# Adding the bias b1 with bfloat16 ones and three bfloat16 parts instead of two fp32r parts

## What is computed

```python
h = jnp.einsum('td,edf->etf', xt, W1) + b1[:, None, :]      # E = 8 experts, D = 128, F = 512
h = _layernorm(jax.nn.relu(h), g1, be1)
y = jnp.einsum('etf,efd->etd', h, W2) + b2[:, None, :]
y = _layernorm(jax.nn.relu(y), g2, be2)
gate = (jax.nn.one_hot(idx, E, dtype=x.dtype) * probs[..., None]).sum(axis=1)   # the two best experts
out = jnp.einsum('te,etd->td', gate, y)
```

## Time and profile before

| | |
|---|---|
| median of three runs | 625.96 us |
| lowest, highest | 620.47, 628.31 us |
| span of the profiled execution | 528.5 us |
| TensorE busy | 492.8 us (93%), mean granted clock 0.965 |
| VectorE busy | 451.7 us (85%) |
| ScalarE busy | 408.1 us (77%) |
| GpSimd busy | 379.2 us (72%) |

### The profile page before, as it was taken

One profiled execution on the slowest core, in us unless ns is written; L12 is line 12 of the kernel. 1 busy time (PEld: TensorE's weight loads), 2 busy tenths in 40 slices (PEclk: granted clock), 3 DMA queues, 4 the chain that ended last, 5 costly groups with the idle time before them and its releaser, 6 DMA issues. The chain is left out here.

```text
span 528.5 us, 15192 instructions
## 1 busy us (share of the span) xinstructions
PE 492.8 (93%) x3105; PEld 392.4 (74%) x3105; DVE 451.7 (85%) x2209; ACT 408.1 (77%) x1115; POOL 379.2 (72%) x523
## 2 busy tenths in 40 slices
PE   7899999999976989999999999989999999999953
PEld 6355666555545879999989889879888888989821
DVE  6778788799995668888999799989999889999887
ACT  7587787868754668888888788888888888888753
POOL 1637777777777776688856578786887777878781
PEclk9999999999985889999999999999999999999986
DMA  6970111155513365555555565665665666665765
GB/s 173 308 215 21 58 52 56 53 134 107 98 56 130 100 150 149 143 153 156 154 146 136 155 175 151 178 190 157 170 196 155 185 190 158 181 193 160 213 174 159
DMA packets 79358, 77.81 MB, mean 147 GB/s; under 512 B 11102, under 2 KB 72697, under 8 KB 79142
## 3 DMA queue, kind: packets, MB, share of 16 engines
q1 hardware_dynamic: 70854, 59.92, 44.5%
q0 software_dynamic: 8416, 16.93, 9.0%
HBM read 54.65 MB, written 22.59 MB: 146 GB/s over the span
## 5 line engine op out<-in xcount | busy, mean ns | idle before, releaser
L602 POOL DMA_INDIRECT expert_rows<-rows_ring,slot x128 | 123.6, 965 | 39.3 <-issue 37.5
L626 POOL DMA_INDIRECT expert_results<-y,target x119 | 118.7, 997 | 36.3 <-issue 35.2
L1530 PE MATMUL bank<-W,h2T 128*128 x1080 | 143.4, 276 | 1.2 <-ACT h2T L792 1.2
L1530 PEld LDWEIGHTS bank<-W,h2T 128*128 128x128 f32 x1080 | 131.9, 193 | 1.6 <-issue 1.6
L784 ACT ACTIVATE h1T<-bank 128x512 f32<-128x512 f32 x135 | 80.7, 598 | 44.7 <-PE bank L1512 42.9
L1287 DVE BATCH_NORM_STATS2 stf<-h1T 128x6 f32<-128x512 f32 x135 | 91.0, 674 | 0.1
L1518 PEld LDWEIGHTS bank<-ident,h1T 128*128 128x128 f32 x540 | 67.7, 141 | 18.7 <-issue 0.4
L1518 PE MATMUL bank<-ident,h1T 128*128 128x128 f32 x540 | 81.3, 273 | 0.0
L792 ACT ACTIVATE h2T<-bank 128x512 f32<-128x512 f32 x135 | 79.5, 589 | 0.1
L1509 PE MATMUL bank<-b_parts,onesr 128*128 x135 | 65.4, 484 | 2.6 <-DVE h3lo L1279 2.4
L701 ACT ACTIVATE n<-X,nm,rs 128x128 f32<-128x128 f32 x128 | 54.0, 483 | 9.0 <-DVE nm L1205 6.9
(11 more groups left out here) (237 smaller groups left out, 1062.2 us busy)
## 6 DMA issues: line engine op xcount, KB each, us to landing
shifts<-expert_shifts SPq DMA_DIRECT2D x119, 192.0 KB
hrow<-expert_rows SPq DMA_DIRECT2D x135, 65.0 KB, 3.0
xi<-expert_results SPq DMA_DIRECT2D x12, 512.0 KB, 5.2
out_x<-X SPq DMA_DIRECT2D x15, 256.0 KB
X<-in_L_attn_x SPq DMA_DIRECT2D x7, 512.0 KB, 7.3
shifts<-in_L_ffn_W SPq DMA_DIRECT2D x4, 512.0 KB, 7.0
expert_rows<-rows_ring,slot POOLq DMA_INDIRECT x128, 2.3
expert_results<-y,target POOLq DMA_INDIRECT x119
```

The lines of the kernel that those rows point to most:

```text
L602: nc.gpsimd.indirect_dma_start(out=rows_d, out_offset=bass.IndirectOffsetOnAxis(ap=slot[q][:, n // TOPK, n % TOPK:n % TOPK + 1], axis=0), ...
L626: nc.gpsimd.indirect_dma_start(out=results_d, out_offset=bass.IndirectOffsetOnAxis(ap=target[i % TARGETS][:], axis=0), in_=y[k], in_offset ...
L1530: ins = mm(acc, rT[q][:, ch * P:(ch + 1) * P], W2[:, bass.ds(e2 * CF + ch, 1), :], start=(ch == 0), stop=(ch == CF - 1))
```

## The change

The ones become the bfloat16 matrix `ones` that other products already use. The table `b1_parts` becomes bfloat16, and three of its rows are filled instead of two: b1 rounded to bfloat16, the rest rounded, and the rest of that, which together are b1 exactly. GpSimd clears the table in one instruction and makes the three parts in four, between its clearing of `b2_rows` and its wait for W1. ScalarE's ten instructions and VectorE's subtraction go. SyncE copies three rows of half the bytes instead of two.

```diff
-        b1hi = sb("b1hi", [E, F], F32R)
-        b1_parts = sb("b1_parts", [P, E, F], F32R)
-        onesr = sb("onesr", [P, P], F32R)
+        PARTS = 3
+        b1_part = [sb(f"b1_part_{n}", [E, F], BF16) for n in range(PARTS)]
+        b1_parts = sb("b1_parts", [P, E, F], BF16)
@@ sync
-            sp.wait_ge(dve_setup, SETUP_END)
-            sp.wait_ge(act_setup, 2)
             sp.wait_ge(b1_zeroed, 1)
-            sp.dma_start(b1_parts[0:1, :, :].bitcast(F32), b1hi[:].bitcast(F32)).then_inc(b1_stored, 16)
-            sp.dma_start(b1_parts[1:2, :, :].bitcast(F32), b1lo[:].bitcast(F32)).then_inc(b1_stored, 16)
+            sp.wait_ge(b1_step, 4)
+            for n in range(PARTS):
+                sp.dma_start(b1_parts[n:n + 1, :, :], b1_part[n][:]).then_inc(b1_stored, 16)
@@ gpsimd
             nc.gpsimd.memset(b2_rows, 0.0).then_inc(b2_zeroed, 1)
+            nc.gpsimd.memset(b1_parts[:].rearrange("p e f -> p (e f)"), 0.0).then_inc(b1_zeroed, 1)
+            pool.wait_ge(gains_loaded, 48)
+            nc.gpsimd.tensor_copy(b1_part[0][:], b1f[:]).then_inc(b1_step, 1)
+            pool.wait_ge(b1_step, 1)
+            nc.gpsimd.tensor_tensor(b1_rest[:], b1f[:], b1_part[0][:], ALU.subtract).then_inc(b1_step, 1)
+            pool.wait_ge(b1_step, 2)
+            nc.gpsimd.tensor_copy(b1_part[1][:], b1_rest[:]).then_inc(b1_step, 1)
+            pool.wait_ge(b1_step, 3)
+            nc.gpsimd.tensor_tensor(b1_part[2][:], b1_rest[:], b1_part[1][:], ALU.subtract).then_inc(b1_step, 1)
@@ scalar
-            act.wait_ge(dve_setup, SETUP_PADDING)
-            for e in range(E):
-                ins = nc.scalar.activation(b1_parts[:, e, :], padding[:, 0:1].broadcast_to([P, F]), ACT.Copy)
-            ins.then_inc(b1_zeroed, 1)
-            def split_b1():
-                act.wait_ge(gains_loaded, 48)
-                act.wait_ge(dve_setup, SETUP_PADDING)
-                nc.scalar.activation(b1hi[:], b1f[:], ACT.Copy).then_inc(act_setup, 1)
-                nc.scalar.activation(onesr[:], onesf[:], ACT.Copy).then_inc(act_setup, 1)
@@ vector, at the end of gains_setup
-                dve.wait_ge(act_setup, 2)
-                mark(vec.tensor_tensor(b1lo[:], b1f[:], b1hi[:], ALU.subtract))
-                assert done[0] == SETUP_END
@@ tensor
-                    mm(h, onesr[:], b1_parts[:, bass.ds(e, 1), :], start=True, stop=False)
+                    mm(h, ones[:], b1_parts[:, bass.ds(e, 1), :], start=True, stop=False)
```

More of the change, by code:

```diff
@@ L140, in adaln_ssm_moe_kernel @@
         scan = [sb(f"scan_{q}", [P, L]) for q in range(2)]
-        spare_gb = [sb("spare_gb_0", [P, L]), sb("spare_gb_1", [P, L], F32R)]
+        spare_gb = [sb(f"spare_gb_{q}", [P, L]) for q in range(2)]
         b1f = spare_gb[0][0:E, :]
-        b1lo = spare_gb[1][0:E, :]
+        b1_rest = spare_gb[1][0:E, :]
         assert L == F
@@ L247, in adaln_ssm_moe_kernel @@
         shift_rows += [of[:, n * 3 * D:(n + 1) * 3 * D] for of in (xi_flat[1], mix_flat) for n in range(2)]
-        shift_rows += [scan[0][:, 0:3 * D], scan[1][:, 0:3 * D], spare_gb[0][:, 0:3 * D], spare_gb[1][:, 0:3 * D].bitcast(F32)]
+        shift_rows += [scan[0][:, 0:3 * D], scan[1][:, 0:3 * D], spare_gb[0][:, 0:3 * D], spare_gb[1][:, 0:3 * D]]
         def ring(i):
@@ L276, in adaln_ssm_moe_kernel @@
         early_gb = [t[:, :].rearrange("p (j d) -> p j d", j=J) for t in scan]
-        second_gb = [t[:, :].bitcast(F32).rearrange("p (j d) -> p j d", j=J) for t in spare_gb]
+        second_gb = [t[:, :].rearrange("p (j d) -> p j d", j=J) for t in spare_gb]
         idle_rows = rows_ring[:].rearrange("p k j r -> p (k j r)")
@@ L303, in adaln_ssm_moe_kernel @@
         gb_stored, gb_loaded, b1_stored = sem("gb_stored"), sem("gb_loaded"), sem("b1_stored")
+        b1_step = sem("b1_step")
         (n1_ready, t1_done, h1T_ready, xi0_done, xi1_done, xi0_ready, xi1_ready, z_done,
@@ L478, in load_shifts @@
                 if i == SLOTS:
-                    sp.wait_ge(b1_stored, 32)
+                    sp.wait_ge(b1_stored, 16 * PARTS)
                 if last_user(i) is not None:
@@ L743, in mixer_step @@
                     normalise(s - 1, n2[1 - q], 0, rs[q], nm[q], range(J // 2, J)).then_inc(n2_ready, 1)
-                if isinstance(s, int) and s == -1:
-                    split_b1()
             run(mixer_step, FIRST1)
@@ L1484, in _ @@
             pe.wait_ge(w1lo_ready, E // W1E)
-            pe.wait_ge(b1_stored, 32)
+            pe.wait_ge(b1_stored, 16 * PARTS)
             pe.wait_ge(table_ready, 1)
@@ L1544, in _ @@
                 mm(late_total[b], ident[:], late_gb[b], start=False, stop=True).then_inc(late_total_done, 1)
-SETUP_PADDING, SETUP_CT, SETUP_MOD, SETUP_GB, SETUP_MIX, SETUP_SUMS, SETUP_END = 2, 3, 4, 8, 12, 13, 14
+SETUP_PADDING, SETUP_CT, SETUP_MOD, SETUP_GB, SETUP_MIX, SETUP_SUMS = 2, 3, 4, 8, 12, 13
 _INS = ['L0_attn_x', 'L0_attn_Win', 'L0_attn_bin_', 'L0_attn_Bp', 'L0_attn_Cp', 'L0_attn_Dp', 'L0_attn_Wout',
```

## The result

The changed kernel takes 630.88 us (median of 10 runs, 626.32 to 637.67), the kernel before 623.69 us (10 runs, 616.60 to 628.31), each run on the same chip. The ratio is 1.0122, 95% interval [1.0087, 1.0157]: some 7.6 us slower, where 1.9 us less were forecast. It is too little for the 2% bound, but it has a sign, and the sign is the other one. Medians here are over all runs of a kernel, ratios and their intervals over its fast runs alone, so that the two need not divide out.

What follows compares the result with a forecast made beforehand. TensorE's products were taken to set the 2.37 us tile period. Product -2.6, waits for rows +0.4 and setup overlap +0.3 sum to -1.9 us against 625.96: 624.1 us (chance 0.73), range 619.5 to 628.1.

Steps and rivals of the forecast that it cites:

- the 2% bound: Whole kernel's time: the change this measurement can tell from none, about 2%, 12.5 us.
- so the work is hidden with 1.3 us to spare: Setup: GpSimd's b1 work ends by 15.4 us, before W1's first cast at 16.71, so it costs nothing there.
- GpSimd's subtractions run beside VectorE's small serial chain: Setup: overlap with VectorE's chain from about 14.67 to 15.4 us costs 0.3 us, bounds 0 to 0.8.
- the setup slips by more than I allow: Setup: what follows if GpSimd's small instructions take twice their price; no size given.
- The product: Expert loop: bfloat16 b1 product saves 16 ns, its weights 3 ns, on each of 135 tiles, 2.6 us.
- the extrapolation from 8 and 32 columns: Expert loop: 0.42 ns a column carried on to 512 columns gives 377 ns for bfloat16 against 393 for fp32r.
- Rival (a): Expert loop: bfloat16 streams no faster in a group with fp32r products; nothing saved, setup costs 0.3, 626.3 us; chance 0.18.
- (b): Expert loop: the b1 product gets much shorter, 13.8 us go, time 612.9 us, just over 2% faster; chance 0.04.
- (c): Expert loop: changing type exposes the next weight load, 0.19 us 135 times, 25.7 us slower, 651 us; chance 0.05.
- What arrives of it: Expert loop: of the product's 2.6 us saving, growing waits for DMA rows take back 0.4 us, TensorE's address instruction zero.
- Waits for rows that grow: Expert loop: some five DMA waits each grow by up to 0.15 us, 0 to 0.8 us, taken as 0.4.

Runs made afterwards that it cites:

- GpSimd's part alone: Kernel before with its fp32r product and two parts, but GpSimd clears the table and does four instructions on b1: 536.25 us, ratio 1.0128.
- its third trace: Trace of the kernel before, run unchanged once more as a sample of TensorE's start: 622.34 us, ratio 1.0074 against itself.
- four products: Product of ones and b1 issued four times a tile, two pairs: fp32r 1.1308 and 1.1188, bfloat16 1.1211 and 1.1080 against the kernel before.
- the product alone: Kernel before with the three-part bfloat16 product, ScalarE clearing and rounding, VectorE subtracting, nothing added to GpSimd: 531.59 us, 1.0038; on another chip 624.63 us, 1.0104.
- the fp32r kernel with four products: Kernel before with its fp32r product of ones and b1 issued four times a tile; second taking 698.56 us, ratio 1.1188.
- the kernel before taken again: Kernel before, unchanged, against itself: 530.78 us, ratio 1.0005.
- the changed kernel with the wait: Changed kernel in which GpSimd's first split of W1 also waits for VectorE's norms of batches 1 and 2: first 629.03 us, 0.9956; again 533.18 us, 1.0042.
- The product alone with the wait: Bfloat16 product with nothing of b1 on GpSimd, and W1's first split also waiting for VectorE's norms, against the kernel before: ratio 0.9984.

## Why the prediction was wrong

**The step that failed** is "so the work is hidden with 1.3 us to spare", on GpSimd's five instructions. It asked when GpSimd's own queue is next needed, and by that it was right (b1 done at 14.36, the cast at 17.14). It did not ask who else is held while GpSimd works. The one place where it did, "GpSimd's subtractions run beside VectorE's small serial chain", took the chain at its old time and 0.3 us for the overlap. The clearing held one VectorE instruction by 2.3 us, b1's subtractions held others, the chain began 3.1 us late, and once late it lay under W1's split, 1.43 + 2.76 us a pair. The price was 6.8 us (4.6 to 8.9), as GpSimd's part alone shows, not 0.3, bounds 0 to 0.8. The last sentence ("the setup slips by more than I allow") came nearest, but for another reason: GpSimd's instructions on b1 took 0.60 and 1.15 us, less than the 0.7 and 1.6 forecast and not twice as much, and the setup slipped all the same.

The prediction had the row for it: VectorE's 0.57 at 24.92, more than three times the 0.17, under this subtraction in the trace of before:

```profile
22.67 2.78 POOL L592 TENSOR_TENSOR W1lo<-shifts,W1hi 128x256 fp32r<-128x256 f32 x4
```

It asked this only of b1's instructions, and not whether the chain stays clear of W1's split. That was the narrow place: the chain ended at 16.5, 0.2 us ahead of a cast at 16.71. The kernel before itself is caught there in its third trace, with the late start: the chain runs from 15.16 to 18.41 us, the cast starts at 16.20, and the steps behind it take 0.31 us. A chain that clears such a neighbour by 0.2 us turns a small delay into a large one.

Under a GpSimd clearing, which reads nothing, VectorE's one-input `TENSOR_SCALAR` was held to its end, while a `BATCH_NORM_AGGREGATE` under it took its 0.38 us. The Trainium skill has this in SBUF — State Buffer, section "Who interferes with whom": the two engines share a pair of ports, `tensor_scalar` may take it whole, and whoever comes second is blocked, not slowed. The trace agrees (2.50 us under the one clearing, 3.53 under a second). The prediction did not weigh this rule, and it speaks against this change.

**The product.** 16 ns from the type and 3 from the weights were forecast; the runs show 18 and some 2, and 20 to 22 ns off the period by the two ways of reading it, 2.7 to 3.0 us in all. That step held, and so did the extrapolation from 8 and 32 columns. Rival (a), no faster in the group, is refuted by the period; (b) and (c) too. (With (c)'s 25.7 us the time would be 651.7, not 651.) The product's row became shorter by far more (0.38 against 0.48), as its wait had moved to the next row.

**What arrives of it** was taken at 2.2 of 2.6 us, and stays open. With four products all of the gain shows in the loop. With one, GpSimd's part with and without the new product gave the same ratio (1.0128 and 1.0127, each known to 0.004, which leaves their difference open by 3 us to either side), and the product alone was 0.4% slower. In the traces of the first kind of chip the loop takes 327.8, 328.2 and 324.9 us with the fp32r product, and 325.2, 324.7, 326.1, 325.7, 327.3 and 326.5 us with the other: 1.1 us less on average, not 2.7 to 3.0. Waits for rows that grow would do this, and the forecast had 0.4 us for them. But the spread within one kind is as large as the difference, the last four of the six come from a chip without a trace of the other product, and no run that loads rows differently was made.

**Open.** The product alone should then be even or 1 to 2 us faster, and its first comparison says 0.1 to 0.7% slower. Its profiled execution had a half-clock stretch at 21 to 24 us (granted 0.50), 1.9 us at the third batch; even so it took 528.93 us, 2.7 under the median, with a span 2.1 us shorter than that of the kernel before taken again (526.8 against 528.9). The stretch is no mark of the new product: the fp32r kernel with four products had one at the same place in its second trace (0.57 from 20 to 24 us, third batch at 28.82). How often the timed runs have it, or the late start, is not known.

No version was faster than the kernel before beyond its interval. The best with the new product that were compared on a chip of the first kind are the product alone and the changed kernel with the wait, both 0.4% slower. The product alone with the wait (0.9984 [0.9919, 1.0050]) was not taken again.

## What to carry to other kernels

Before giving GpSimd work "in idle time", list VectorE's instructions in that time too: here a `TENSOR_SCALAR` or two-input step that started under a GpSimd instruction often lasted until that one ended. Price the delay at the first reader of VectorE's result, and look for what stands right behind the chain; here 3 us of delay became 6. A gain of 1% of a tile's period showed in the period at once, and in the time could not be told from nothing; multiplying the changed instruction by four made it measurable.

## What was not expected of the hardware

- GpSimd cleared 128 x 4096 in bfloat16 in 3.50 us, 0.85 ns an element, and in GpSimd's part alone as many in float32 in the same time: half the bytes gave nothing.

```profile
4.41 3.50 POOL L580 MEMSET b_parts<- 128x4096 f32 x1
```

- The TensorE of one program can stay at half its clock until 7 us in one execution and until 15 us in another: six transposes take 1.65 us against 0.94. The view's granted clock doesn't show it, since its records begin with the rise.
- fp32r products of 512 columns take 232 ns a slot and bfloat16 ones 214, inside one accumulation; the change of type in it costs nothing that shows.
- The same program takes 530 us on some chips and 620 to 630 on others. On the slower kind the loop over batches ends 250.9 instead of 177.6 us into the changed kernel, with a median tile period of 2.353 or 2.354 us on both.
